# One fused transformer layer: the turn of the next pair's x is issued ahead of the first sequence's values, and its cast ahead of the heads

## The chip, the core and the metric

The kernel runs on one NeuronCore of a Trainium2 chip. The metric is device time in microseconds (us), lower is better: the median of the kernel before is 1051.24 us over 3 runs (1051.01 to 1052.17). The engines are TensorE (PE in the profile; PEld is its weight load, which overlaps the matmuls), VectorE (DVE), ScalarE (ACT), GpSimd (POOL) and SyncE (SP), which issues the transfers.

## The reference

The layer takes x of shape 64 x 256 x 192. A token mixer turns each group of 16 tokens into 8, so that a sequence of 256 becomes one of 128. Then come attention (12 query heads, 3 key and value heads of 64, rotary embedding, a window that covers all 128 tokens) and a feed-forward block with 768 hidden units, each behind a layer norm and with a residual.

```python
h = tok(x, Wq, bq, Wkv, bkv)               # (64, 256, 192) -> (64, 128, 192)
h = h + attention(layernorm(h), Wq, Wk, Wv, Wo)
h = h + gelu(layernorm(h) @ in_weight.T + in_bias) @ out_weight
```

The token mixer is itself a small attention inside each group:

```python
q = (xv @ Wq.T + bq) * scale               # 8 new tokens of a group, over d = 192
k, v = split(xv @ Wkv.T)                   # v has the bias bkv
out = q.T + softmax(q k) v
```

## The kernel before, in words

The 64 sequences go through as 32 pairs; in a pair the sequences are a = 0 and a = 1. The program is written out by hand, engine by engine, with semaphores. Every engine runs the same function `step(p, att, tok, ffn, fin)` for p from -1 to 33; 2 to 30 are one loop. A step holds four stages of a software pipeline: attention of pair p (`att`), the token mixer of pair n = p + 1 (`tok`), the first feed-forward product and the Gelu of pair p - 1 with the rest of its attention (`ffn`), and the second feed-forward product of pair p - 2 (`fin`). All four are there in p = 2 to 30; p = 1 lacks only `fin`; p = 0 has `att` and `tok`; p = 31 has no `tok`.

An engine works through its instructions in the order written, and an instruction that waits for a semaphore holds back what is written behind it. So the order in `step` sets the order of the work. What the change touches is the last part of a step. On PE it is, in order:

- `ffn_first` (L732): the first feed-forward product, 30 matmuls.
- `probs_v(0, p)` (L717): probabilities times values of sequence 0, in two parts. The first part gives 512 columns, the second 256, and each counts up `pv_mm`. The probabilities come back through DRAM (`spill`, then `ET`), and `filled` says that they are there.
- `x_turned` (L805): four transposes of `xn`, the normalised input of the next pair, into PSUM bank 7 (`B7`). Two of them wait for each sequence's `xn_out`, which DVE counts up in `normalise` (L468).
- `output(0, p)` (L824): six fp32 matmuls of the heads `OT` with `wo_sb`. The first four wait for the first half of `OT`, the last two for the second.

Then the next step begins with `qkv(0)` (L670), which waits for `XH` and `XL`, the turned x split into a rounded part and a rest. ACT casts `XH` from `B7` (L359), and DVE subtracts to get `XL` (L646). ACT also copies the heads from PSUM to `OT` in `heads_out` (L306), one copy for each part of `probs_v`, and after that runs the Gelu of the feed-forward block.

DVE's part ahead of `xn` is: the statistics of `h_next`, the row maxima of the scores, the reciprocal of the first sums, and then the two `normalise` calls (two instructions each, L470 and L472). The scale `rs1` comes from POOL (L425), which after it goes on to multiply the probabilities (L403).

Of the kernel before, what the change touches and what calls it, by code (L numbers as in the profile page):

```python
# [82 lines left out]
def program(nc, x, w_tok, b_tok, bq_row, w_att1, w_att2, wo, w_in1, w_in2, b_in, w_out,  # L83
# [4 lines left out]
    with ExitStack() as ctx:  # L88
# [188 lines left out]
        def _(act):  # L277
# [12 lines left out]
            def step(p, att, tok, ffn, fin):  # L290
                n = p + 1
                def qk_turned(a):
                    for b in range(2):
                        c = slice(512 * b, 512 * (b + 1))
                        act.wait_ge(qT_mm, 4 * p + 2 * a + b + 1)
                        nc.scalar.copy(qkT[:, a, c], RING[a][:, c]).then_inc(qT_out, 1)  # L296

                def score_exp(a, k):
                    g = GROUPS[k]
                    act.wait_ge(max_out, 6 * p + 3 * a + k + 1)  # L300
                    for s in range(REP * g, REP * (g + 1)):
                        last = nc.scalar.activation(E[:, a, s * P:(s + 1) * P], RING[a][:, s * P:(s + 1) * P], ACT.Exp,  # L302
                                                    bias=m_neg[:, a, s:s + 1], accum_out=e_sum[:, a, s:s + 1])
                    last.then_inc(exp_out, 1)

                def heads_out(a, q):  # L306
                    for b, c in enumerate((slice(0, 512), slice(512, DQ))):
                        heads = (c.stop - c.start) // P
                        act.wait_ge(pv_mm, 4 * q + 2 * a + b + 1)
                        nc.scalar.copy(OT[:, a, c].rearrange("p (h i c) -> p h i c", h=heads, i=NB),  # L310
                                       RING[a][:, c].rearrange("p (i h c) -> p h i c", h=heads, i=NB)).then_inc(OT_out, 1)

                def tok_vq(i):
                    act.wait_ge(vq_mm, 2 * n + i + 1)
                    for k, (dst, bias) in enumerate(((t_v, bias_rows[:, 1:2]), (t_q, bias_sc[:]))):
                        r0 = (i ^ k) * (P // 2)
                        rows = slice(r0, r0 + P // 2)
                        nc.scalar.activation(dst[rows], TOK_VQ[i][rows].rearrange("p (a d) -> p a d", a=2),
                                             ACT.Identity, bias=bias[rows]).then_inc(vq_out, 1)

                if att:
                    act.wait_ge(s_warm_exp, p + 1)
                    nc.scalar.activation(warm[:, 1:2], half_neg[:, 0:1], ACT.Exp).then_inc(s_warm_exp, 1)
                    qk_turned(0)
                if tok:
                    if isinstance(p, int) and p == -1:
                        act.wait_ge(s_scaled, 4)
                    tok_vq(0)
                    tok_vq(1)
                if att:  # L330
                    score_exp(0, 0)
                if ffn:
                    heads_out(1, p - 1)
                if att:
                    score_exp(0, 1)
                    score_exp(0, 2)
                if tok:
                    act.wait_ge(s_max, n + 1)
                    for a in range(2):
                        nc.scalar.activation(t_e[:, a, :], t_s[:, a, :], ACT.Exp, bias=t_neg[:, a:a + 1],  # L340
                                             accum_out=t_sum[:, a:a + 1]).then_inc(t_exp, 1)
                    act.wait_ge(t_rcp, n + 1)
                    for a in range(2):
                        nc.scalar.activation(t_a[:, a, :], t_e[:, a, :], ACT.Copy,
                                             scale=t_rs[:, a:a + 1]).then_inc(t_norm, 1)
                    act.wait_ge(aT_mm, n + 1)
                    nc.scalar.copy(t_aT[:].rearrange("p a c -> p (a c)"), TOK_AT).then_inc(aT_out, 1)
                if att:
                    qk_turned(1)
                if ffn:  # L350
                    act.wait_ge(hT_mm, p)
                    nc.scalar.copy(HH[:].rearrange("p c a t -> p (c a t)"), B7[:]).then_inc(HH_out, 1)  # L352
                if att:
                    for g in range(NKV):
                        score_exp(1, g)
                    heads_out(0, p)
                if tok:
                    act.wait_ge(xT_mm, n + 1)
                    nc.scalar.copy(XH[:].rearrange("p a c -> p (a c)"), B7[:]).then_inc(XH_out, 1)  # L359
                    if isinstance(p, int) and p == -1:  # L360
                        act.wait_ge(s_w3, 16 * 5)
                        nc.scalar.copy(FH1[:], win_raw[:, 0:HID]).then_inc(s_hi, 1)
                        nc.scalar.copy(F2S[:], win_raw[:, HID:2 * HID]).then_inc(s_hi, 1)
                if ffn:
                    act.wait_ge(s_warm, p)
                    nc.scalar.activation(warm[:, 0:1], warm[:, 0:1], ACT.Gelu).then_inc(s_warm, 1)
                    for m in (2 * j + i for j in GELUS for i in range(2)):
                        act.wait_ge(hid_mm, 3 * (p - 1) + m // 2 + 1)
                        nc.scalar.activation(G[:, m, :], HIDDEN[m // 2][:, (m % 2) * DP:(m % 2 + 1) * DP], ACT.Gelu,  # L369
                                             bias=b_hid[:, m:m + 1]).then_inc(gelu_out, 1)  # L370

            run(act, step)

        @block.gpsimd
# [284 lines left out]
        def _(pe):  # L659
# [6 lines left out]
            def step(p, att, tok, ffn, fin):  # L666
# [50 lines left out]
                def probs_v(a, q):  # L717
                    if tok and a == 1:
                        pe.wait_ge(tqk_out, n + 1)
                    first_8 = ET[:, a, 0:8 * P].rearrange("p (i h c) -> p i h c", i=NB, h=8)  # L720
                    last_4 = ET[:, a, 8 * P:NH * P].rearrange("p (i h c) -> p i h c", i=NB, h=4)
                    for b, halves in enumerate((((0, first_8[:, :, 0:4]), (1, first_8[:, :, 4:8])),
                                                ((2, last_4[:, :, 0:2]), (2, last_4[:, :, 2:4])))):
                        pe.wait_ge(filled[b], 64 * (2 * q + a + 1))
                        n_cols = (512, 256)[b]
                        for k, (g, src) in enumerate(halves):
                            last = nc.tensor.matmul(RING[a][k * HD:(k + 1) * HD, 512 * b:512 * b + n_cols],  # L727
                                                    v_tok[:, a, g * HD:(g + 1) * HD], src.rearrange("p i h c -> p i (h c)"),
                                                    start=True, stop=True)
                        last.then_inc(pv_mm, 1)  # L730
# [74 lines left out]
                def x_turned():  # L805
                    for a in range(2):
                        pe.wait_ge(xn_out, 2 * n + a + 1)
                        nc.tensor.transpose(B7[:, a * DP:a * DP + P], xn[:, a, 0:P], ident[:])
                        last = nc.tensor.transpose(B7[:, a * DP + P:(a + 1) * DP], xn[:, a, P:DP], ident[:])
                    last.then_inc(xT_mm, 1)  # L810
# [13 lines left out]
                def output(a, q):  # L824
                    if first == "att":
                        pe.wait_ge(s_w3, 16 * 5)
                    if a == 0:
                        pe.wait_ge(exp_out, 6 * q + 6)
                    else:
                        pe.wait_ge(h2_out, 2 * q + 1)  # L830
                    for t in range(6):
                        if t % 4 == 0:
                            pe.wait_ge(OT_out, 4 * q + 2 * a + t // 4 + 1)
                        last = nc.tensor.matmul(ATT_Y, OT[:, a, t * P:(t + 1) * P], wo_sb[:, t, :],  # L834
                                                start=(t == 0), stop=(t == 5))
                    last.then_inc(y_mm, 1)
# [42 lines left out]
                    scores(1)  # L879
                if ffn:  # L880
                    ffn_first()
                if att:
                    probs_v(0, p)
                if tok:
                    x_turned()
                if att:
                    output(0, p)

            run(pe, step)


# [39 lines left out]
```

## Time and profile before

| | value |
|---|---|
| median of 3 runs | 1051.24 us |
| profiled execution, its own time | 1053.71 us |
| its span | 1051.8 us |
| PE busy | 998.5 us (95%) |
| PE weight load busy | 866.3 us (82%) |
| DVE busy | 814.6 us (77%) |
| ACT busy | 733.9 us (70%) |
| POOL busy | 435.2 us (41%) |
| mean granted clock of TensorE | 0.982 of full speed |

In the lists of rows below, times are microseconds from the start of the span. The number behind "x" at the end of a row is how many instructions were merged into it; an fp32 matmul stands in the profile as two. A bracket at the end of a row holds the idle time of the engine ahead of it and what ended it.

### The profile page before, as it was taken

To read this page: it belongs to the slowest core of one execution; us is meant where nothing else is said; L and a number is where in the kernel's file an instruction comes from. 1 tells how busy PE (TensorE), PEld (TensorE's weight loads), DVE (VectorE), ACT (ScalarE), POOL (GpSimd) and SP (SyncE) were. 2 spreads that over 40 slices of the span, in tenths; PEclk is the share of its full clock that TensorE was granted. 3 is DMA by queue.
4 is the path that set the end of the run, shared out by engine and by line. 5 is a ranking of instruction groups with operands and counts; after the bars stand their busy time and mean duration, and the time that the engine had idled before them with its cause. 6 is when DMAs were issued, how large, how long until landed. Compare 5 with 4: busy or idle time off the path is not lost. (4 is left out here: it accounts for less than half of the span.)

```text
span 1051.8 us, 24498 instructions
## 1 busy us (share of the span) xinstructions
PE 998.5 (95%) x7232; PEld 866.3 (82%) x7232; DVE 814.6 (77%) x2095; ACT 733.9 (70%) x2530; POOL 435.2 (41%) x583
## 2 busy tenths in 40 slices
PE   3689999999999999999999999999999999999987
PEld 2577888888988888888888888888889888888865
DVE  2678888778878877888877888887788787788861
ACT  2456777777776677677777777677867777777761
POOL 0334444443544343454444444434345444434440
PEclk7789999999999999999999999999999999999999
DMA  5134434334434434443433454343444344334331
GB/s 174 43 106 134 133 107 143 117 110 127 147 118 116 138 109 118 136 142 110 130 124 106 125 147 126 108 142 112 118 130 146 116 119 132 111 113 146 115 112 45
DMA packets 139935, 127.49 MB, mean 121 GB/s; under 512 B 30992, under 2 KB 123024, under 8 KB 139920
## 3 DMA queue, kind: packets, MB, share of 16 engines
q1 hardware_dynamic: 137632, 124.16, 39.5%
q10 hardware_dynamic: 2288, 3.15, 0.9%
q8 instruction: 7, 0.11, 0.0%
q14 instruction: 8, 0.07, 0.0%
HBM read 70.63 MB, written 56.62 MB: 121 GB/s over the span
## 5 line engine op out<-in xcount | busy, mean ns | idle before, releaser
L403 POOL TENSOR_TENSOR E<-E,e_rcp 128x512 f32<-128x512 f32 x192 | 198.7, 1042 | 284.7 <-DVE e_rcp L534 281.6
L302 ACT ACTIVATE E<-ring,m_neg 128x128 f32<-128x128 f32 x768 | 272.0, 389 | 56.3 <-DVE m_neg L514 56.3
L395 POOL TENSOR_TENSOR q_tok<-rot_c,rot_s 128x384 f32<-128x384 f32 x128 | 125.8, 1005 | 132.7 <-DVE rot_s L492 132.7
L302 ACT ACTIVATION_READ_ACCUMULATOR E<-ring,m_neg 128x1 f32 x768 | 174.7, 227 | 0.0
L514 DVE TENSOR_REDUCE m_neg<-ring 128x4 f32<-128x512 f32 x192 | 122.7, 681 | 57.0 <-PE ring L710 57.0
L296 ACT COPY qkT<-ring 128x512 f32<-128x512 f32 x128 | 71.9, 588 | 128.3 <-PE ring L689 128.3
L525 DVE STREAM_TRANSPOSE EB<-E 128x512 f32<-128x512 f32 x192 | 134.3, 699 | 17.7 <-POOL E L403 17.7
L834 PE MATMUL ring<-wo_sb,OT 128*128 128x192 f32 x768 | 139.6, 332 | 1.5 <-ACT OT L310 1.5
L697 PE MATMUL bank<-wout_sb,G 128*128 128x192 f32 x768 | 135.4, 326 | 2.8 <-ACT G L369 2.8
L697 PEld LDWEIGHTS bank<-wout_sb,G 128*128 128x128 f32 x768 | 125.4, 190 | 3.4 <-ACT G L369 3.3
L834 PEld LDWEIGHTS ring<-wo_sb,OT 128*128 128x128 f32 x768 | 124.1, 191 | 3.9 <-issue 2.4
L710 PEld LDWEIGHTS ring<-qkT 64*128 64x128 f32 x1536 | 91.9, 190 | 29.8 <-ACT qkT L296 29.8
L710 PE MATMUL ring<-qkT 64*128 64x128 f32 x1536 | 104.3, 283 | 5.0 <-ACT qkT L296 1.4
L727 PE MATMUL ring<-ET,v_tok 128*64 128x512 f32 (+1 forms) x512 | 97.0, 499 | 1.1 <-DMA ET<-spill 1.1
L490 DVE TENSOR_TENSOR rot_c<-ring,rope_qc 128x384 f32<-128x384 f32 x128 | 69.9, 546 | 14.9 <-issue 12.2
L663 PE MATMUL ring<-WH,XH 128*128 128x384 f32 x192 | 73.8, 384 | 1.5 <-DVE XL L646 1.5
L492 DVE TENSOR_TENSOR rot_s<-ring,rope_qs 128x384 f32<-128x384 f32 x128 | 69.9, 546 | 0.0
L727 PEld LDWEIGHTS ring<-ET,v_tok 128*64 128x64 f32 x512 | 31.0, 136 | 46.4 <-issue 36.2
L689 PE MATMUL ring<-ident,q_tok 128*128 128x128 f32 x384 | 60.1, 279 | 8.3 <-POOL q_tok L395 8.3
L663 PE MATMUL ring<-W2S,XL 128*128 128x384 f32 x192 | 65.4, 341 | 0.0
L663 PE MATMUL ring<-W2S,XH 128*128 128x384 f32 x192 | 65.2, 340 | 0.0
L663 PE MATMUL ring<-WL,XH 128*128 128x384 f32 x192 | 65.2, 339 | 0.0
(122 smaller groups left out, 2275.9 us busy)
## 6 DMA issues: line engine op xcount, KB each, us to landing
spill<-EB SPq DMA_DIRECT2D x64, 512.0 KB, 2.7
ET<-spill SPq DMA_DIRECT2D x256, 128.0 KB, 2.8
spill<-EB SPq DMA_DIRECT2D x64, 256.0 KB, 2.1
ET<-spill SPq DMA_DIRECT2D x256, 64.0 KB, 2.3
x_sb<-in_x_dram SPq DMA_DIRECT2D x64, 192.0 KB, 2.5
out_dram<-out_sb SPq DMA_DIRECT2D x64, 96.0 KB, 2.3
x_sb<-in_x_dram SPq DMA_DIRECT2D x64, 64.0 KB, 2.3
w_raw<-in_w_att_dram ACTq DMA_DIRECT2D x2, 576.0 KB, 4.8
```

Source lines behind the costliest of these rows:

```text
L296: nc.scalar.copy(qkT[:, a, c], RING[a][:, c]).then_inc(qT_out, 1)
L302: last = nc.scalar.activation(E[:, a, s * P:(s + 1) * P], RING[a][:, s * P:(s + 1) * P], ACT.Exp, bias=m_neg[:, a, s:s + 1], accum_out=e_s ...
L395: nc.gpsimd.tensor_tensor(q_tok[:, a, c], rot_c[:, a, c], rot_s[:, a, c], ALU.add).then_inc(q_out, 1)
L403: nc.gpsimd.tensor_tensor(e, e, r, ALU.mult).then_inc(prob_out, 1)
L490: nc.vector.tensor_tensor(rot_c[:, a, c].rearrange("p (h d) -> p h d", d=HD), src.rearrange("p (h d) -> p h d", d=HD), cos, ALU.mult)
L514: nc.vector.tensor_reduce(m_neg[:, a, REP * g:REP * (g + 1)], RING[a][:, 512 * g:512 * (g + 1)].rearrange("p (h k) -> p h k", k=P), AX_X, ...
L525: nc.vector.transpose(EB[:, a, s0 * P:(s0 + heads) * P].rearrange("p (j h c) -> p h j c", j=NB, h=heads)[:, h0:h0 + REP], E[:, a, 512 * g: ...
L663: last = nc.tensor.matmul(out_ap, lhsT, rhs, start=(i == 0), stop=(i == len(terms) - 1))
L697: last = nc.tensor.matmul(B6[:, a * D:(a + 1) * D], G[:, m, a * P:(a + 1) * P], wout_sb[:, m, :], start=(m == 0), stop=(m == NM - 1))
L710: last = nc.tensor.matmul(RING[a][:, s * P:(s + 1) * P], qkT[rows, a, t * P:(t + 1) * P], qkT[rows, a, k0:k0 + P], start=True, stop=True)
L727: last = nc.tensor.matmul(RING[a][k * HD:(k + 1) * HD, 512 * b:512 * b + n_cols], v_tok[:, a, g * HD:(g + 1) * HD], src.rearrange("p i h c ...
L834: last = nc.tensor.matmul(ATT_Y, OT[:, a, t * P:(t + 1) * P], wo_sb[:, t, :], start=(t == 0), stop=(t == 5))
```

## The change

On PE, `x_turned` goes ahead of `probs_v(0, p)`, so that values and output of sequence 0 follow on one another. On ACT, the cast of `XH` goes ahead of `heads_out(0, p)`. Nothing is added or taken away, and DVE, POOL and SP keep their order.

```diff
@@ ScalarE, step @@
                 if att:
                     for g in range(NKV):
                         score_exp(1, g)
-                    heads_out(0, p)
                 if tok:
                     act.wait_ge(xT_mm, n + 1)
                     nc.scalar.copy(XH[:].rearrange("p a c -> p (a c)"), B7[:]).then_inc(XH_out, 1)
...
+                if att:
+                    heads_out(0, p)
                 if ffn:
                     act.wait_ge(s_warm, p)
@@ TensorE, step @@
                 if ffn:
                     ffn_first()
+                if tok:
+                    x_turned()
                 if att:
                     probs_v(0, p)
-                if tok:
-                    x_turned()
-                if att:
                     output(0, p)
```

TensorE at the end of the loop's step, before the change: the last matmul of `ffn_first` (HL with F2S), the values (ET with v_tok), the turn of x (ident with xn), the output (wo_sb with OT), and the next `qkv(0)` (WH with XH).

```order
L748 MATMUL ring<-HL,F2S 128x256
L727 MATMUL ring<-ET,v_tok 64x512 x2
L727 MATMUL ring<-ET,v_tok 64x256 x2
L808 MATMUL bank<-ident,xn 128x128
L809 MATMUL bank<-ident,xn 128x128
L808 MATMUL bank<-ident,xn 128x128
L809 MATMUL bank<-ident,xn 128x128
L834 MATMUL ring<-wo_sb,OT 128x192 x6
L208 UNCONDITIONAL_BRANCH
L208 ISA
L663 MATMUL ring<-WH,XH 128x384
```

The four transposes stand between the values and the output. The same place after the change, where line numbers from 363 on are one higher:

```order
L749 MATMUL ring<-HL,F2S 128x256
L809 MATMUL bank<-ident,xn 128x128
L810 MATMUL bank<-ident,xn 128x128
L809 MATMUL bank<-ident,xn 128x128
L810 MATMUL bank<-ident,xn 128x128
L728 MATMUL ring<-ET,v_tok 64x512 x2
L728 MATMUL ring<-ET,v_tok 64x256 x2
L835 MATMUL ring<-wo_sb,OT 128x192 x6
L208 UNCONDITIONAL_BRANCH
L208 ISA
L664 MATMUL ring<-WH,XH 128x384
```

The transposes now follow `ffn_first` directly, and the output follows the values with nothing between. ScalarE behind the exponentials of sequence 1 (E), before the change; OT are the heads, XH is the cast of the turned x:

```order
L302 ACTIVATE E,e_sum<-ring,m_neg 128x128 x4
L310 COPY OT<-ring 128x512
L310 COPY OT<-ring 128x256
L359 CAST XH<-bank 128x512
L366 ACT_TABLE_LOAD
```

and after it:

```order
L302 ACTIVATE E,e_sum<-ring,m_neg 128x128 x4
L358 CAST XH<-bank 128x512
L310 COPY OT<-ring 128x512
L310 COPY OT<-ring 128x256
L367 ACT_TABLE_LOAD
```

The cast has changed places with the two copies, and the table load for the Gelu stays behind all three.

## Rows read from the trace of the kernel before

**Rows 1.** Page, part 1: busy us, share of the span, instructions.

```profile
PE 998.5 (95%) x7232; PEld 866.3 (82%) x7232; DVE 814.6 (77%) x2095; ACT 733.9 (70%) x2530; POOL 435.2 (41%) x583
```

**Rows 2.** Stretches of PE: from:to, length, busy (instructions), granted clock, DMA share, GB/s.

```profile
498.56:529.55 30.99, 30.67 (x228) 1.00 0.43 125
62.00:64.00 2.00, 1.84 (x6) 0.50 0.00 0
82.00:86.00 4.00, 2.56 (x15) 1.00 0.67 232
```

**Rows 3.** Timeline of PE, step's end: start, us, line, tiles, count.

```profile
525.60 0.28 PE L748 MATMUL ring<-HL,F2S 128*128 128x256 f32 x1
525.80 1.51 PE L727 MATMUL ring<-ET,v_tok 128*64 128x512 f32 x8
527.24 0.33 PE L808 MATMUL bank<-ident,xn 128*128 128x128 f32 x1
527.41 0.27 PE L809 MATMUL bank<-ident,xn 128*128 128x128 f32 x1
527.52 0.27 PE L808 MATMUL bank<-ident,xn 128*128 128x128 f32 x1
...
527.74 2.12 PE L834 MATMUL ring<-wo_sb,OT 128*128 128x192 f32 x12
529.55 0.47 PE L663 MATMUL ring<-WH,XH 128*128 128x384 f32 x1
```

**Rows 4.** DVE by line and shape, 93 to 993 us: count, busy us, mean ns, idle before.

```profile
L514 DVE TENSOR_REDUCE m_neg<-ring 128x4 f32<-128x512 f32 x174 | 111.2, 681 | 51.3 <-PE ring L710 51.3
```

**Rows 5.** Timeline of DVE at the step's end.

```profile
524.63 1.22 DVE L470 TENSOR_SCALAR xn<-h_next,mv,rs 128x192 f32<-128x192 f32 x1
525.77 0.30 DVE L472 TENSOR_SCALAR xn<-h_next,mv,rs 128x64 f32<-128x64 f32 x1
525.99 0.37 DVE L470 TENSOR_SCALAR xn<-h_next,mv,rs 128x192 f32<-128x192 f32 x1
526.28 0.30 DVE L472 TENSOR_SCALAR xn<-h_next,mv,rs 128x64 f32<-128x64 f32 x1
...
528.55 0.69 DVE L646 TENSOR_TENSOR XL<-bank,XH 128x512 fp32r<-128x512 f32 x1
```

**Rows 6.** DVE by line and shape again, both halves of xn's first instruction.

```profile
L470 DVE TENSOR_SCALAR xn<-h_next,mv,rs 128x192 f32<-128x192 f32 x58 | 46.0, 794 | 0.5
```

**Rows 7.** Timeline of DVE at the end of p = 0.

```profile
62.06 0.30 DVE L472 TENSOR_SCALAR xn<-h_next,mv,rs 128x64 f32<-128x64 f32 x1
```

**Rows 8.** Timeline of PE at the end of p = 0.

```profile
62.42 0.48 PE L808 MATMUL bank<-ident,xn 128*128 128x128 f32 x1
62.69 0.42 PE L809 MATMUL bank<-ident,xn 128*128 128x128 f32 x1
63.27 3.17 PE L834 MATMUL ring<-wo_sb,OT 128*128 128x192 f32 x12 [0.16 <-ACT OT L310]
```

**Rows 9.** Timeline of PE in p = 31 and p = 32.

```profile
1019.79 1.51 PE L727 MATMUL ring<-ET,v_tok 128*64 128x512 f32 x8
1021.64 2.19 PE L834 MATMUL ring<-wo_sb,OT 128*128 128x192 f32 x12 [0.34 <-ACT OT L310]
...
1028.64 1.08 PE L727 MATMUL ring<-ET,v_tok 128*64 128x512 f32 x4 [0.89 <-DMA ET<-spill]
```

**Rows 10.** Timeline of ACT in p = 32.

```profile
1029.77 0.59 ACT L310 COPY OT<-ring 128x512 f32<-128x512 f32 x1 [4.29 <-PE ring L727]
```

**Rows 11.** Timeline of ACT at the step's end of group 3.

```profile
526.63 0.24 ACT L302 ACTIVATION_READ_ACCUMULATOR E<-ring,m_neg 128x1 f32 x1
526.93 0.86 ACT L310 COPY OT<-ring 128x512 f32<-128x512 f32 x2
527.94 0.59 ACT L359 CAST XH<-bank 128x512 fp32r<-128x512 f32 x1
528.54 1.28 ACT L366 ACT_TABLE_LOAD   x1
```

**Rows 12.** Timeline of POOL at the same place.

```profile
524.69 1.04 POOL L403 TENSOR_TENSOR E<-E,e_rcp 128x512 f32<-128x512 f32 x1
```

More of the change, by code:

```diff
@@ L881, in step @@
                     ffn_first()
-                if att:
-                    probs_v(0, p)
                 if tok:
@@ L886, in step @@
                 if att:
+                    probs_v(0, p)
                     output(0, p)
```

## The prediction

> **What bounds the kernel now.** I read the page's busy times first, then PE's busy time over one step, then the timelines of the step's end, engine by engine. PE is busy for 95% of the span [rows 1]. One whole step of the loop, from the first matmul of `qkv(0)` to the next one, lasts 30.99 us, and PE is busy for 30.67 of them at the full granted clock [rows 2]. So in the steady loop only 0.32 us of a step are left to gain, and whatever makes PE wait longer lengthens the step. At the step's end PE runs without a wait: the last row of the first feed-forward product at 525.60, the values at 525.80, the turn of x at 527.24, the output at 527.74, the next `qkv(0)` at 529.55 [rows 3]. From the values to the next step that is 3.75 us. DVE has room: in the middle of each of 29 steps it waits for PE's scores, 51.3 us together, 1.77 us a step [rows 4]. That wait also means that DVE's delay against PE is made anew in every step and not carried over.
>
> **The change, first term: x is not ready so early.** Nothing is added, so all cost is in waits. The transposes move from 527.24 to the place of the values. PE comes to them at about 525.8, where the values start now [rows 3]. Their input is not there. The second sequence's `xn` ends at 526.28 + 0.30 = 526.58 [rows 5]. This step is no exception: its two L470 rows, 1.22 and 0.37 us, have a mean of 0.795, and the 58 of 29 steps have 0.794 [rows 5, 6]. What DVE does up to there follows PE's scores of sequence 1 and does not depend on what is moved. In p = 0, where PE already waits for x, the second `xn` ends at 62.06 + 0.30 = 62.36 [rows 7] and the second pair of transposes starts at 62.42 [rows 8]: 0.06 us later. So in the loop it would start at 526.64. The first transpose of a pair takes 0.17 us to the next, the second 0.11 (527.24, 527.41, 527.52) [rows 3], so the values start at 526.92 instead of 525.80: 1.12 us later, of which 0.50 us are the transposes themselves, taken from behind the values.
>
> **Second term: the heads' copy lies bare.** Before, the transposes ran between values and output while ACT copied the heads. Now nothing does. The trace shows this order once, in p = 31, which has no turn of x: values at 1019.79, output at 1021.64, so 1.85 us, with PE idle 0.34 us for the copy [rows 9]. In p = 32 ACT was idle ahead of the copy, and it starts 1.13 us after the first values (1028.64 to 1029.77) and lasts 0.59 us [rows 9, 10]; with 0.06 us to PE that is 1.78. I take 1.85, since p = 31 has the whole sequence in one piece. The output then starts at 526.92 + 1.85 = 528.77. Its rows last 2.19 us behind a wait and 2.12 without one [rows 3, 9], so the stretch from output to `qkv(0)` becomes 1.81 + 0.07 = 1.88 us and the next step starts at 530.65 instead of 529.55. That is 1.10 us per step.
>
> **What is moved besides, at nothing.** On ACT the cast waits for the transposes. Before, it began 0.42 us behind the second pair (527.52 to 527.94) [rows 3, 11]; now that gives 527.06 to 527.65. The exponentials end at 526.87, and the copies are not due before 526.92 + 1.13 = 528.05, so ACT is free for both. Queued behind the waiting cast are the two copies, the table load and the Gelu. The copies end at 528.05 + 0.86 = 528.91, so the table load goes from 528.54 to about 528.9, 0.4 us later, while PE's next use of the Gelu moves by 1.1: covered. Without that cover it would cost up to 0.4 us a step. `XL` gains nothing: it stands behind DVE's own transposes, starts at 528.55 and ends at 529.24 [rows 5], which was already 0.31 us ahead of the next `qkv(0)`. Its slack grows to 1.4 us and buys no time. The transfers of `ET` show no wait in the loop, and the later values only ease them; SP's queue is not touched.
>
> **The rest of the program.** The loop's order holds in p = 1 to 30, 30 steps: 30 x 1.10 = 33.0 us. In p = 0 the second pair starts at 62.42 either way and steps by 0.27 us there, at the lower clock, 1.2 GHz (0.50 in 62 to 64 us) [rows 2, 8]. Values at 62.96 and output 1.85 us later, at 64.81, against 63.27: 1.5 us. If the values run at half clock too, up to 1.4 us more (an estimate: their 1.51 us nearly twice); if the output by then has the full clock, 3.17 - 2.19 = 0.98 us less [rows 8, 9]. So 0.6 to 2.9, and I take 1.5. p = -1 and p = 31 keep their order. Sum: 34.5 us. The profiled execution took 1053.71 us (span 1051.8), so it would take 1088.2. That execution stands 2.5 us above the median of 1051.24, and to the median the sum gives 1085.7; I say 1086.
>
> Bounds of a step: if each transpose needs only 0.11 us, the output comes after 1.78 us and its 0.07 are not paid, the next step starts at 526.64 + 0.22 + 1.78 + 1.81 = 530.45, +0.90. If the values need 0.1 us behind the transposes and the copy's hand-over another 0.1, it is +1.3. That is 27 to 39 us, and with p = 0 a time of 1079 to 1093.
>
> **Rivals.** *x in time (1068 us).* The 1.22 us of the first `xn` instruction lie over POOL's multiplication from 524.69 to 525.73 [rows 5, 12], and it ends just behind it; its twin takes 0.37. If DVE ran first, both halves would be done 0.85 us earlier, at 525.73, and the transposes would not wait. The values would start at 525.80 + 0.50 = 526.30, the output at 528.15, the next step at 530.03 (ACT, done with its cast at 527.46, would add 0.03). That is 0.5 us a step, 15 + 1.5 us. Against it: the slow form stands in all 29 steps [rows 6], and neither engine's order ahead of it changes. The Trainium skill, page "SBUF — State Buffer", section "Who interferes with whom", says that the two engines share a pair of ports as an exclusive lock and whoever issues first holds it for the whole instruction. By that rule, read on the listed starts (524.63 for DVE, 524.69 for POOL), DVE should hold it and this rival come true; the trace agrees on the lock and shows it with POOL.
>
> *Not slower (1052 us).* DVE's delay could be backlog. Once PE has fallen behind by a microsecond, x would always be in time, and the 0.32 us of waits that a step holds today [rows 2] would go, since DVE, POOL and ACT would all be ahead. Against that stands the copy's wait alone, at its lowest row 0.34 us [rows 9]: 30 x 0.02 + 0.6 = 1.2 us. It decides from the point where DVE no longer waits for PE in mid-step; with 1.77 us of such wait in each step [rows 4] there is no backlog to work off.
>
> *The clock falls (1158 us).* If a wait of 0.6 and one of 0.4 us at the step's end cost the full clock there, values and output would take nearly 1.4 and 1.05 us more (3.17 against 2.12 [rows 3, 8]), some 2.4 us in each of 30 steps. Against it: from 82 to 86 us PE was busy 2.56 of 4 us and the clock stayed at 1.00 [rows 2], with longer idle time than this.
>
> That the change does nothing is excluded: PE and ACT issue in the order written, and the order of both has changed.
>
> **How the numbers follow.** Forecast 0.88, x in time 0.06, not slower 0.03, clock 0.03. Less than 0.2%, about 2.1 us, can't be told from no change here. Faster needs a step under 31 us without either wait, which no row allows: 0.02. Same is the not-slower case with its p = 0: 0.03. Slower is the rest, 0.95. The range of 1077 to 1094 is the forecast's with its bounds and 1 to 2 us for the spread of the runs; the other cases, 0.12, lie outside.
>
> **What would show it.** In the profile after: a step of 32.1 us; PE idle some 0.6 to 0.9 us ahead of the second pair of transposes, released by DVE's `xn`; PE idle about 0.35 us ahead of the output, released by ACT's copy of the heads; `XL` ending more than 1 us before `qkv(0)`; a granted clock of 1.00 in the loop. A first `xn` instruction of 0.37 us would prove the first rival. The forecast is wrong if a step stays at 31 us, or if PE waits at a third place.

## The result

The changed kernel takes 1088.26 us (median of 4 runs, 1088.12 to 1088.62) against 1051.12 us for the kernel before: a ratio of 1.0354, 95% interval 1.0336 to 1.0372. It is slower by 37 us; its profiled execution took 1088.18 us, with a span of 1086.3 us against 1051.8. Two executions of the experiments below (3472.29 us with TensorE's part alone, 1149.40 us with half of the turn) ran in a slower state and are left out of the times given, as they are of the ratios.

The busy times on the page have hardly moved: PE 1011.4 us against 998.5 [rows 1], and the same number of instructions. (PE's busy time is modelled and includes the ends of pipelined matmuls, which lie bare where PE waits.)

One whole step of the loop, from one `qkv(0)` to the next (columns as in [rows 2]):

```profile
548.83:580.95 32.12, 31.11 (x229) 1.00 0.40 120
```

A step lasts 32.12 us instead of 30.99 (31.00 over many), and 1.01 us of it are idle instead of 0.32. The granted clock in it is 1.00. The whole span, from the `qkv(0)` of p = 1 to that of p = 2, from there to that of p = 31, and from there to the end, first in the kernel before and then in the changed kernel (columns as in [rows 2]):

```profile
66.14:95.58 29.44, 27.60 (x205) 1.00 0.39 112
95.58:994.55 898.97, 889.83 (x6556) 1.00 0.41 124
994.55:1051.77 57.22, 44.99 (x296) 0.97 0.31 93
```

```profile
67.42:99.27 31.85, 29.30 (x205) 0.95 0.36 108
99.27:1030.51 931.24, 902.77 (x6556) 1.00 0.40 120
1030.51:1086.31 55.80, 43.39 (x296) 0.99 0.30 86
```

The 29 steps from p = 2 to p = 30 lose 32.3 us, 1.11 each. What stands ahead of p = 1 loses 1.3 us (66.14 to 67.42). The step p = 1 loses 2.4 us, and 1.1 of them are no wait: the granted clock fell in it to the lower level, 1.2 GHz, and PE's work from the first turn of q to the scores took 4.31 us (84.61 to 88.92) instead of 3.17 (83.36 to 86.53). At the end the changed kernel is 1.4 us shorter, because there the clock fell in the kernel before (0.51 from 1038 to 1041 us). Together that is 34.5 us. The fall in p = 1:

```profile
86.00:88.00 2.00, 2.00 (x10) 0.50 0.95 264
```

The step's end on PE, which answers to [rows 3]:

```profile
543.66 0.28 PE L749 MATMUL ring<-HL,F2S 128*128 128x256 f32 x1
544.20 0.33 PE L809 MATMUL bank<-ident,xn 128*128 128x128 f32 x1 [0.26 <-DVE xn L473]
544.37 0.27 PE L810 MATMUL bank<-ident,xn 128*128 128x128 f32 x1
544.71 0.14 PEld L809 LDWEIGHTS bank<-ident,xn 128*128 128x128 f32 x1 [0.31 <-DVE xn L473]
544.71 0.33 PE L809 MATMUL bank<-ident,xn 128*128 128x128 f32 x1
...
544.88 0.27 PE L810 MATMUL bank<-ident,xn 128*128 128x128 f32 x1
...
545.08 1.51 PE L728 MATMUL ring<-ET,v_tok 128*64 128x512 f32 x8
546.94 2.19 PE L835 MATMUL ring<-wo_sb,OT 128*128 128x192 f32 x12 [0.34 <-ACT OT L310]
```

Both waits are there. The transposes wait for DVE twice: the first pair with a bracket of 0.26 us; the second, from 544.37 to 544.71, with none on its matmul, because the modelled end of the matmul ahead covers the gap, but with one of 0.31 us on its weight load. And the output waits 0.34 us for ACT's copy. DVE in the same place, to [rows 5]:

```profile
542.70 1.22 DVE L471 TENSOR_SCALAR xn<-h_next,mv,rs 128x192 f32<-128x192 f32 x1
...
544.35 0.30 DVE L473 TENSOR_SCALAR xn<-h_next,mv,rs 128x64 f32<-128x64 f32 x1
...
546.53 0.65 DVE L647 TENSOR_TENSOR XL<-bank,XH 128x512 fp32r<-128x512 f32 x1
```

The first `xn` instruction is again the slow one of 1.22 us, and the second `xn` ends at 544.65, 0.06 us before its transposes. `XL` ends at 547.18, now 1.65 us before it is needed. And ACT, to [rows 11]:

```profile
545.19 0.59 ACT L358 CAST XH<-bank 128x512 fp32r<-128x512 f32 x1 [0.24 <-PE bank L810]
546.21 0.86 ACT L310 COPY OT<-ring 128x512 f32<-128x512 f32 x2 [0.43 <-PE ring L728]
```

ACT is idle ahead of the cast and ahead of the copies: the copy begins 1.13 us after the first values (545.08), as it did in p = 32 before [rows 9, 10].

### The profile page after: what moved, and what is told of

Read it like the earlier page. It is cut to its first block and busy times, and to the rows that moved or that the text cites. A ratio compares the mean times of both kernels' runs of the same rounds, so it can differ in the third digit from the quotient of the medians.

```text
span 1086.3 us, 24498 instructions
## 1 busy us (share of the span) xinstructions
PE 1011.4 (93%) x7232; PEld 867.2 (80%) x7232; DVE 810.9 (75%) x2095; ACT 734.1 (68%) x2530; POOL 435.0 (40%) x583
## 5 line engine op out<-in xcount | busy, mean ns | idle before, releaser
L404 POOL TENSOR_TENSOR E<-E,e_rcp 128x512 f32<-128x512 f32 x192 | 198.6, 1041 | 282.2 <-DVE e_rcp L535 279.2
L539 DVE TENSOR_TENSOR h<-ring,h_cur 128x192 f32<-128x192 f32 x64 | 22.9, 359 | 63.7 <-PE ring L835 63.7
L310 ACT COPY OT<-ring 128x512 f32<-128x512 f32 (+1 forms) x128 | 55.6, 491 | 18.9 <-PE ring L728 18.9
L664 PE MATMUL ring<-WH,XL 128*128 128x384 f32 x192 | 65.2, 340 | 0.0
```

The lines of the kernel that those rows point to most:

```text
L404: nc.gpsimd.tensor_tensor(e, e, r, ALU.mult).then_inc(prob_out, 1)
L664: last = nc.tensor.matmul(out_ap, lhsT, rhs, start=(i == 0), stop=(i == len(terms) - 1))
```

## The experiments

The theory was the prediction's: TensorE now waits twice in each step, for the second `xn`, and for the heads' copy, which no longer has work of TensorE beside it. The rivals were that ScalarE's new order is the cause, that only one of the waits costs, or that the new order costs something in itself. Ratios are against the kernel before on the same chip, with their 95% intervals.

**TensorE's part alone.** ScalarE keeps its old order, copies ahead of the cast.

```diff
                     for g in range(NKV):
                         score_exp(1, g)
+                    heads_out(0, p)
...
-                if att:
-                    heads_out(0, p)
```

> TensorE's part of the change alone: the turn of x ahead of the values, while ScalarE keeps the heads' copies ahead of the cast. Theory (two waits of TensorE, for xn and for the copy of the heads): ScalarE is idle when either is due, so its order costs nothing; the cast comes after the copies at about 0.5 us ahead of need. 1088 us, 1084 to 1092, a step of 32.1 us, with the same two waits. Rival (the cast ahead of the heads is what delays the heads): most of the loss is gone, 1051 to 1070 us.

Measured: 1086.90 us, ratio 1.0339 (1.0316 to 1.0361), a step of 32.11 us. ScalarE's half of the change costs and saves nothing in the new kernel. Its cast there, behind the copies, and DVE behind it:

```profile
545.80 0.60 ACT L359 CAST XH<-bank 128x512 fp32r<-128x512 f32 x1
```

```profile
546.43 0.69 DVE L646 TENSOR_TENSOR XL<-bank,XH 128x512 fp32r<-128x512 f32 x1 [0.98 <-ACT XH L359]
```

`qkv(0)` starts at 547.67. So the cast comes 1.8 us later in the step than in the changed kernel (1.87 us ahead of `qkv(0)` instead of 3.64), and `XL`, which ends at 547.12, still has 0.55 us to spare.

**ScalarE's part alone.** TensorE keeps its old order; the cast goes ahead of the copies.

> ScalarE's part alone: the cast ahead of the heads' copies, TensorE's order as before the change. Theory: the copies now queue behind a cast that waits for the transposes; the first copy starts about 1.6 us later (528.5 instead of 526.93 in the step shown), the output 1.5 us later, a step of 32.5 us, 1099 us (1092 to 1106), with no wait for xn. Rival (the order of ScalarE is off the critical path, as its 70% busy time suggests): 1051 us.

Measured: 1096.26 us, ratio 1.0416 (1.0397 to 1.0435), a step of 32.40 us (522.21 to 554.61). On ACT and on PE:

```profile
519.10 0.59 ACT L358 CAST XH<-bank 128x512 fp32r<-128x512 f32 x1 [1.07 <-PE bank L810]
519.59 0.87 ACT L310 COPY OT<-ring 128x512 f32<-128x512 f32 x2
```

```profile
520.32 2.19 PE L835 MATMUL ring<-wo_sb,OT 128*128 128x192 f32 x12 [1.25 <-ACT OT L310]
```

ACT sits idle for 1.07 us in front of a cast whose transposes are not done, with copies queued behind it that could have run, and TensorE waits 1.25 us for them. So the heads' copy is on the path, and an engine that is busy 70% of the time still sets the pace by its order.

**x in time, in the changed kernel.** DVE normalises ahead of the reciprocal that sets off POOL's multiplication.

```diff
-                if att:
-                    sums_inverted(1, 0, p)
                 if tok:
                     dve.wait_ge(ln1_rs, n + 1)
...
                         normalise(h_next, mv1, rs1, xn, a).then_inc(xn_out, 1)
                 if att:
+                    sums_inverted(1, 0, p)
                     sums_inverted(1, 1, p)
```

> The changed kernel, with VectorE normalising x ahead of the reciprocal of the first sums, so that GpSimd's multiplication no longer runs over it. Theory: the first xn instruction falls from 1.22 to 0.37 us, the second xn is done 0.85 us earlier, the wait for x goes, the wait for the heads stays at 0.34 us: a step of 31.5 us, 1069 us (1065 to 1074). Rival 1 (only the lateness of x costs): 1051 to 1055 us. Rival 2 (the transposes wait for something else than VectorE): 1088 us.

Measured: 1063.34 us, ratio 1.0111 (1.0092 to 1.0129); a step of 31.35 us. Timelines of DVE and PE:

```profile
530.31 0.38 DVE L471 TENSOR_SCALAR xn<-h_next,mv,rs 128x192 f32<-128x192 f32 x1
...
531.12 0.30 DVE L473 TENSOR_SCALAR xn<-h_next,mv,rs 128x64 f32<-128x64 f32 x1
```

```profile
531.29 0.28 PE L748 MATMUL ring<-HL,F2S 128*128 128x256 f32 x1
531.41 0.28 PE L808 MATMUL bank<-ident,xn 128*128 128x128 f32 x1
...
531.63 0.27 PE L808 MATMUL bank<-ident,xn 128*128 128x128 f32 x1
...
531.94 1.51 PE L727 MATMUL ring<-ET,v_tok 128*64 128x512 f32 x8
533.80 2.19 PE L834 MATMUL ring<-wo_sb,OT 128*128 128x192 f32 x12 [0.35 <-ACT OT L310]
535.69 0.47 PE L663 MATMUL ring<-WH,XH 128*128 128x384 f32 x1
```

The `xn` instruction falls from 1.22 to 0.38 us, the wait for x is gone, the wait for the copy stays. That splits the loss of a step: 32.12 - 31.35 = 0.77 us are x, 31.35 - 31.00 = 0.35 us the rest, net of 0.09 us that are given back elsewhere (below). The time lies 2 us under the expected range; the transposes are 0.11 us apart when nothing holds them, where 0.17 had been read for the first of a pair.

**Control: the same DVE move in the kernel before.**

> Control for the last: the kernel before with the same move on VectorE. Theory: TensorE does not wait for x there, and the later probabilities have slack: 1051 us, within 2 us, although the xn instruction falls to 0.37 us. If it is faster or slower by more, the effect of the move itself must be taken off the last run.

Measured: 1052.45 us, ratio 1.0004 (0.9993 to 1.0014): no difference, although the instruction takes 0.38 us there too. What the last run gained is not the move's own. In this profile the clock falls in p = 1 as well (0.50 from 85 to 88 us), with TensorE's order as before the change: the new order is not needed for it.

**Half of the turn ahead.** In the kernel before, the first sequence's two transposes go ahead of the values; the second's stay.

```diff
+                if tok:
+                    x_turned((0,))
                 if att:
                     probs_v(0, p)
                 if tok:
-                    x_turned()
+                    x_turned((1,))
```

> The kernel before with only the first sequence's half of the turn moved ahead of the values; the second half stays between values and output, ScalarE keeps the heads' copies ahead of the cast. Theory (each wait is priced by when its own input is ready): the first half waits for the first xn, about 0.35 us, so the values start 0.70 us later; the second half finds its xn ready and covers part of the copy, so that the output waits at most 0.1 us: a step of 31.55 us, 1069 us (1064 to 1073). Rival (the waits come with any move of x ahead of the values, whole): 1088 us. Rival (only the bare copy costs): 1051 to 1055 us.

Measured: 1072.14 us, ratio 1.0200 (1.0182 to 1.0218), a step of 31.59 us.

```profile
535.80 0.33 PE L808 MATMUL bank<-ident,xn 128*128 128x128 f32 x1 [0.25 <-DVE xn L472]
...
536.17 1.51 PE L727 MATMUL ring<-ET,v_tok 128*64 128x512 f32 x8
537.61 0.33 PE L808 MATMUL bank<-ident,xn 128*128 128x128 f32 x1
...
538.02 2.19 PE L835 MATMUL ring<-wo_sb,OT 128*128 128x192 f32 x12
```

The half that goes ahead waits for its own `xn`; the half that stays does not. From values to output it is again 1.85 us (536.17 to 538.02): two transposes in the gap cost nothing, because the copy sets that time.

**The copy covered by other work.** On top of x in time, the last 3 of the 30 feed-forward matmuls move between values and output.

```diff
                 if att:
                     probs_v(0, p)
+                    if ffn:
+                        ffn_first(True)    # the last 3 of 30 matmuls
                     output(0, p)
```

> The kernel with x in time (the changed order, xn ahead of the first reciprocal), and the last 3 of the 30 matmuls of the first feed-forward product moved from ahead of the turn of x to between values and output: 0.36 us of work that has nothing to do with the heads. Theory (what is left of the loss is the heads' copy with nothing of TensorE's beside it): any work there covers it, the step falls from 31.35 to about 31.0 us, 1051 to 1054 us, with the turn of x still ahead of the values. Rival (the rest is a price of the new order itself, of the hand-over between transposes and values or of the copies behind the cast): 1061 to 1065 us as without the move.

Measured: 1061.08 us, ratio 1.0080 (1.0064 to 1.0095), a step of 31.27 us. By the number the rival would have it. The rows say something else:

```profile
529.76 0.27 PE L815 MATMUL bank<-ident,xn 128*128 128x128 f32 x1
530.09 0.33 PE L814 MATMUL bank<-ident,xn 128*128 128x128 f32 x1
...
531.90 0.38 PE L753 MATMUL ring<-HH,F2S 128*128 128x256 f32 x1
...
532.36 2.14 PE L840 MATMUL ring<-wo_sb,OT 128*128 128x192 f32 x12
```

The output follows the moved matmuls without a wait, so the copy is covered. But the transposes come 0.36 us earlier for it, and the second pair waits again (529.76 to 530.09, where 0.11 is free running). My expectation left out that x was in time by only 0.15 us in the run before. It settles nothing by its time alone.

**The copy shortened.** So the copy itself was made shorter, with TensorE's order left as it was.

```diff
+                        if a == 0 and b == 0:
+                            nc.scalar.copy(dst[:, 0:1], src[:, 0:1]).then_inc(OT_first, 1)
+                            h0 = 1
+                        nc.scalar.copy(dst[:, h0:], src[:, h0:]).then_inc(OT_out, 1)
...
+                        if a == 0 and t == 0:
+                            pe.wait_ge(OT_first, q + 1)
```

> The kernel with x in time (the changed order, xn ahead of the first reciprocal), and ScalarE's first copy of the heads of sequence 0 divided: 128 of its 512 columns first, with a semaphore of their own that the first output matmul waits for, then the other 384. The last run covered the copy but brought the turn of x 0.36 us forward and so let a wait for xn return; here nothing on TensorE moves. Theory (what is left of the loss is the length of the copy): the first output starts about 0.3 us earlier, the second waits at most 0.1 us, a step of 31.35 us falls to 31.05 to 31.1 us, 1055 us (1053 to 1058). Rival (the price is that of the hand-overs in the new order, not of the copy): 1062 to 1065 us, as without the division.

Measured: 1054.29 us, ratio 1.0035 (1.0024 to 1.0045), a step of 31.02 us (532.11 to 563.13).

```profile
529.81 0.27 ACT L314 COPY OT<-ring 128x128 f32<-128x128 f32 x1
```

```profile
528.04 0.28 PE L753 MATMUL ring<-HL,F2S 128*128 128x256 f32 x1
...
528.69 1.51 PE L732 MATMUL ring<-ET,v_tok 128*64 128x512 f32 x8
530.22 2.19 PE L841 MATMUL ring<-wo_sb,OT 128*128 128x192 f32 x12
532.11 0.47 PE L668 MATMUL ring<-WH,XH 128*128 128x384 f32 x1
```

From values to output it is 1.53 us instead of 1.86. The step's end, from the last feed-forward row to `qkv(0)`, now prices the two waits: 5.17 us in the changed kernel, 4.40 with x in time, 4.07 with the short copy too, 3.95 before [rows 3]. So of 1.22 us x is 0.77 and the copy 0.33; 0.12 remain with the new order, and what they are made of was not tried apart. The step of 31.02 us is that of the old order, to 0.02 us, only because 0.09 us come back elsewhere (next). The whole kernel is 4 us slower than the kernel before on its chip; the loop's steps are under 1 us of that, and where the rest lies is not shown.

**The 0.09 us given back.** From the last feed-forward row to the next `qkv(0)` the changed kernel takes 1.22 us more (543.66 to 548.83), but the step grows by only 1.12. The rest comes back in the mixer's first four small matmuls. Kernel before, then changed kernel, both PE:

```profile
532.31 0.69 PE L763 MATMUL ring<-bd_qk,x_sb 128*128 128x128 f32 x4
532.83 1.06 PE L767 MATMUL ring<-bd_qk,x_sb 128*128 128x128 f32 x8
```

```profile
551.58 0.61 PE L764 MATMUL ring<-bd_qk,x_sb 128*128 128x128 f32 x4
552.02 1.06 PE L768 MATMUL ring<-bd_qk,x_sb 128*128 128x128 f32 x8
```

0.52 us against 0.44. They wait for the last Gelu, which before ends at 532.23 and in the changed kernel at 550.77. Two runs tested this. The first put these matmuls behind the second feed-forward product:

> The kernel before with the mixer's queries and keys (tok_qk) issued behind the second feed-forward product of sequence 0 instead of ahead of it. Theory: the 0.08 us that the changed kernel gives back in each step are a wait of tok_qk's first weight load for the last Gelu, which ends at 532.23, just as tok_qk begins at 532.31; here it has 2 us to spare, so the step falls from 31.00 to 30.92 us, 29 steps, 1049 us. Rival (the 0.08 us are an effect of what stands ahead of them on TensorE): 1051 to 1052 us.

Measured: 1051.92 us, ratio 1.0004 (0.9989 to 1.0019). The expectation rested on an oversight: the second feed-forward product waits for the same Gelu, so the wait only changed its owner (its first six matmuls took 2.03 us instead of 1.96). The second run ended the Gelu earlier by joining its last two instructions; it leaves out the bias of the last 128 hidden units and gives them that of the 128 before.

> The kernel before with the last two Gelus of a step joined into one instruction of 512 columns with the bias of the first of the two (so the hidden units 640 to 767 get the bias of 512 to 639): the last Gelu ends 0.1 to 0.2 us earlier. Theory (0.07 to 0.08 us of each step before are the mixer's first weight load, or what stands first, waiting for the last Gelu): a step of 30.92 us, tok_qk's first four rows take 0.44 instead of 0.52 us, 1048.5 to 1050 us. Rival (no wait for the Gelu; the last run only moved something else): a step of 31.00 us and 0.52 us as before.

Measured: 1049.89 us, ratio 0.9979 (0.9970 to 0.9988), a step of 30.92 us (528.80 to 559.72):

```profile
531.55 0.61 PE L768 MATMUL ring<-bd_qk,x_sb 128*128 128x128 f32 x4
531.99 1.06 PE L772 MATMUL ring<-bd_qk,x_sb 128*128 128x128 f32 x8
```

0.44 us, as in the changed kernel, and the Gelu now ends 0.22 us ahead of them (at 531.33), where it was 0.08. So the kernel before held a wait that no bracket showed. Its weight loads do show it, by their starts:

```profile
531.96 0.19 PEld L663 LDWEIGHTS ring<-W2S,XL 128*128 128x128 f32 x1
532.28 0.52 PEld L763 LDWEIGHTS ring<-bd_qk,x_sb 128*128 128x128 f32 x4
```

From one load to the next it is 0.32 us; in the changed kernel, 0.18 (551.23 to 551.41).

**A kernel faster than both.** If waits on TensorE are what counts, those that the kernel before still has are worth taking away. This run is built on the one with the mixer's queries and keys behind the second feed-forward product ("the last kernel" of its expectation); that part of its edit is not repeated here.

```diff
                 if att:
-                    blocks_turned(0, 1, p)
...
                     rotate(1, (0, 1))
-                    blocks_turned(0, 2, p)
+                    blocks_turned(0, 1, p)
                     rotate(1, (2,))
                     keys_added(1)
...
                     normalise(h2, mv2, rs2, hn, 1).then_inc(hn_out, 1)
                 if att:
+                    blocks_turned(0, 2, p)
                     v_out_of_psum(1)
@@ TensorE @@
-                if tok:
-                    tok_h()
                 if att:
                     qk_turned(1, (6, 7))
+                if tok:
+                    tok_h()
```

> The last kernel, and the two waits left in a step taken away as well: on VectorE the rotation of sequence 1 and hn go ahead of two transposes of probability blocks, so that q_tok and k_tok are ready earlier (0.19 us), and on TensorE the mixer's h goes behind the turn of the keys, where it lies beside the copy of qkT that the scores wait for (0.12 us). Theory: where TensorE is the bound, each wait taken away is time: a step of 30.6 to 30.7 us, 1041 to 1045 us. Rival 1 (the chain from x to XL, which ended 0.3 us ahead of the next qkv, becomes the bound): 1046 to 1049 us. Rival 2 (the later blocks bring ET late to the values): slower than 1051 us, with a wait for ET.

Measured: 1044.79 us, ratio 0.9939 (0.9923 to 0.9955), a step of 30.79 us (columns as in [rows 2]):

```profile
494.26:525.05 30.79, 30.54 (x228) 1.00 0.42 126
```

0.21 us a step are gained instead of 0.3 to 0.4; a wait of 0.25 us for `k_tok` is left, and the Gelu's is still there (2.04 us for the first six matmuls of the second product). Which of the moves brought how much was not tried apart.

## Why the prediction was right

**The bound.** That a step had 0.32 us to lose and every new wait would be paid held: the loop's loss is 1.11 to 1.12 us a step, 1.10 was forecast. Only the 0.32 us were not the whole room: with the last Gelus joined, a step is shorter by 0.08 us and its idle time is still 0.31, since PE was listed as busy in that wait.

**First term, x not ready.** The second pair was to start 1.04 us after the last feed-forward row (526.64 - 525.60) and starts 1.05 us after it (544.71 - 543.66). The values were to start 0.28 us behind that and start 0.37 us behind: the hand-over from transposes to values takes 0.20 us, as from feed-forward to values, and not 0.11. That was one of the upper bounds. The experiment with x in time prices the lateness at 0.77 us. The sign given for it came otherwise than written: not 0.6 to 0.9 us ahead of the second pair, but 0.42 ahead of the first (0.54 behind the last feed-forward row, where 0.12 is free running) and 0.23 ahead of the second (0.34, where 0.11 is).

**Second term, the bare copy.** From values to output 1.85 us were forecast and 1.86 came; from output to `qkv(0)` 1.88, and 1.89 came. Shortening the copy took 0.33 us of the price back.

**What was costed at nothing.** ScalarE's order, `XL` and the later table load held. One edit at nothing was not nothing: the later use of the Gelu gave back 0.09 us. It offset the 0.09 us by which the first term was short. That the step came out right to 0.02 us is luck.

**p = 0.** In the forecast 1.5 us. The second pair of transposes stands 3.72 us before the next `qkv(0)` in the kernel before (62.42 to 66.14) and 5.26 us in the changed one, where the pair itself comes 0.26 us earlier:

```profile
62.16 0.48 PE L809 MATMUL bank<-ident,xn 128*128 128x128 f32 x1
...
62.78 2.54 PE L728 MATMUL ring<-ET,v_tok 128*64 128x512 f32 x8
65.53 2.19 PE L835 MATMUL ring<-wo_sb,OT 128*128 128x192 f32 x12 [0.20 <-ACT OT L310]
```

That is 1.54 us, with the values slow (2.54 us instead of 1.51) and the output fast (2.19 instead of 3.17), as the two bounds had it; 1.03 us more and 0.98 less cancelled.

**The rivals.** x in time did not come by itself, but it was made to happen: 1063 us where the rival said 1068. In that run POOL's multiplication starts at 531.59, behind the end of the second `xn` at 531.42, so it shows what the instruction takes with POOL idle. The Trainium skill, page "SBUF — State Buffer", section "Who interferes with whom", says that whoever issues first holds the shared ports; this run does not test that, and the 31 steps in which POOL starts 0.06 us behind DVE and DVE takes 1.22 us go against it, if the listed starts are the order of issue. Not slower: DVE still waits for PE in mid-step, 48.9 us over 29 steps where it was 51.3 [rows 4], and nothing was worked off. The clock stayed at 1.00 in the loop from p = 2 on. In p = 1 it fell (0.50 from 86 to 88 us), right behind the place (82 to 86 us) whose row the prediction had cited against this rival, and cost 1.1 us.

The 1086 us forecast lie 2.3 us under the measured 1088.26; 34.5 us were summed, and the spans differ by 34.5. That match is partly luck too: each of the two profiled executions has one stretch of lower clock that the other lacks, and their 1.1 and 1.4 us nearly cancel. The medians differ by 37.1 us. The prediction took 2.5 us off for the distance of the profiled execution from the median, but that distance belonged to the one execution of the kernel before, which the stretch at its end had lengthened by 1.4 us; the changed kernel's profiled execution stands at its median (1088.18 and 1088.26).

## What to carry to other kernels

Where one in-order engine bounds the kernel, look up for each instruction that is moved ahead when its input is ready, and for each one that it leaves behind, which wait it had been covering: here four transposes were cheap filler for a copy's latency, and became a wait of their own in the new place. The order on an engine with idle time counts as much, if it puts something that waits in front of something that could run. A wait that is taken away shows the next one's slack, so read that slack before counting the gain.

## What the runs showed of the hardware that was not expected

A wait can be hidden in PE's rows. The mixer's four matmuls took 0.52 us behind a Gelu that ended just ahead of them, and 0.44 with the Gelu done earlier, without a bracket; only the starts of the weight loads show it. The same `xn` instruction takes 1.22 us when POOL's multiplication is listed as starting 0.06 us after it, and 0.38 us when that comes later: the listed order of starts did not tell which engine would be held. And the granted clock fell to about half for some 3 us in p = 1 of the changed kernel and at the end of the kernel before, at a cost of 1.1 and 1.4 us, with 1.00 from p = 2 to p = 30 in both.
